# Norm factors of a recurrent attention layer: their rows read ahead of the weight loads, sums of squares taken two pairs at a time, first type's factors applied ahead of the chunk mask

## The chip, the cores and the metric

One NeuronCore of a Trainium2 chip runs the whole program. The time is the device time of one launch in microseconds (us). Before the change three runs took 3392.41, 3395.30 and 3405.55 us, median 3395.3 us.

## The reference, cut to what matters

The layer is x += 0.5 FFN(LN(x)); x += attention(LN(x)); x += 0.5 FFN(LN(x)), for x of 4 sequences x 512 tokens x 256 features. The FFN is a mixture of 64 experts with 8 chosen per token. The change touches only the attention layer, a gated linear recurrence over 64 heads with a state of 128 x 8 per head:

```
Bm = rmsnorm((x @ WB.T)) * Bn_w + B_bias      # 64 heads x 128 entries per token
Cm = rmsnorm((x @ WC.T)) * Cn_w + C_bias      # rmsnorm(v) = v * rsqrt(mean(v*v) + 1e-6), per head
Bm, Cm = rope(Bm, cumsum(theta*dt)), rope(Cm, cumsum(theta*dt))
h_t = alpha_t h_{t-1} + beta_t B_{t-1} x_{t-1} + gamma_t B_t x_t ;   y_t = C_t h_t
y = (y * silu(z)) @ Wout.T
```

B and C are the two "types". Each head of each type needs one norm factor per token, 1/sqrt(mean of squares + eps).

## The kernel before, in words

The program runs the first FFN, then the attention of the four sequences one after the other (scans 0 to 3), and the second FFN. The routing of the second FFN begins between scans. Each scan has a preparation (`prep_*`) and then 32 turns, one for each pair of heads; a turn is one pass of the loop body of `turn_pe`, `turn_act`, `turn_dve`, `turn_pool` and `turn_sp`, written out four times (j = 0 to 3) inside a loop of eight. Each engine runs its own list in a written order, and semaphores tie the lists together: `e_*` are raised by engines and `a_*` by landed DMAs. Work for several pairs is in flight. In turn n, TensorE does in this order: the sums of squares of pair n+2 (`ss_pe`, L1220), the outputs of pair n-2 (`Y_pe`, L1414 and L1416), the chunk products of pair n-1 (`G_pe`, L1350), its transposes (L1359), half of the B/C projection of pair n+3 (`A_pe`, L64), the chunk states of pair n-1 (`K2_pe`, L1390), the other half of the projection, and the angle projection of pair n+2 (`T_pe`, L64). VectorE does: angle scaling (L1171) and scan (L1174) of pair n+1, the decay scan of pair n (L1280), L1285, L1180, then `K_dve1` (the mask on the chunk products, L1374), in odd turns `Y_dve` (L1428, L1432), then `F_dve1` (the norm factors times B, then times C, both L1274), in odd turns `R_dve` (a reciprocal, L1250), the four rope multiplies `F_dve3` (L1298), and the state scan `K_dve2` (L1399). GpSimd follows with L1306 and L1307, which finish the rotated B and C that `G_pe` of the next turn reads.

The norm factors travel once per two pairs. After the second `ss_pe` of a group (odd turn), ScalarE takes the square root (`R_act`, L1238). A DMA turns the 8 rows of 512 into a 128 x 32 tile (`R_rows`, L1245, rc_in), VectorE takes the reciprocal (L1250), a DMA writes it to DRAM (`R_sp2`, L1255, rr_dram), and once that has landed two DMAs read it back, broadcast over the partitions (`R_sp3`, L1264, rr_bc, 2 x 512 KB). The next turn, an even one, begins `F_dve1` with these factors.

All loads of scans 1 to 3 are issued by SP, in one list and on one DMA queue. An odd turn's SP list is: dt rows, end rows (L1149), th load (L1055, 256 KB), wb load (L1047, 1024 KB), `R_rows`, al rows (L1149, 2 x 128 KB), `R_sp2`, `R_sp3`. In scan 0 the weights come from another array, are split into a high and a low part on ScalarE and VectorE, and `R_rows` is issued by ScalarE on its own queue, as in the changed kernel; only L1255 and L1264 are SP's there.

The sums of squares are matmuls of a 128 x 32 one-hot slice with a 128 x 512 tile of squares. Each writes one of two 32-row column groups of one PSUM bank, two matmuls (even and odd entries) for B and two for C per pair. The square root's target, `stdr`, is a slice of the tile `decay_t`.

## Time and profile before

| | |
|---|---|
| median of 3 runs | 3395.3 us (3392.41 to 3405.55) |
| the profiled execution | 3382.4 us, span 3380.6 us |
| granted TensorE clock, mean over the span | 0.909 |
| TensorE busy | 2799.0 us, 83% |
| VectorE busy | 2326.1 us, 69% |
| ScalarE busy | 1816.0 us, 54% |
| GpSimd busy | 1501.2 us, 44% |
| data moved | 609.71 MB, mean 180 GB/s |

The four scans lie from about 590 us to about 2900 us. The mean shares mix them with the two FFNs and with the stretches between scans, so the argument reads the steady part of the scans by itself. Times in timelines are microseconds from the start of the span; DMA rows show when the issuing queue worked, not when the data landed.

### The profile page before, as it was taken

The numbers are of one execution on the slowest core, as the hardware profiler recorded it, in microseconds if no ns is written. First come the engines' busy times: TensorE is split into PE (matmuls) and PEld (weight loads), VectorE is DVE, ScalarE is ACT, GpSimd is POOL, SyncE is SP. The second block draws the span as 40 slices with busy tenths as digits, with TensorE's granted clock in tenths as the row PEclk, the third lists the DMA queues.
The fourth block names the chain that finished last, engine by engine and source line by source line (L and its number), as shares of the span: only waits on it lengthen the run. The fifth ranks groups of instructions, "written<-read, shape, count | busy, mean of one in ns | idle before, by whom it ended". The sixth has DMA issues, their size and how long they took to land.

```text
span 3380.6 us, 83925 instructions
## 1 busy us (share of the span) xinstructions
PE 2799.0 (83%) x28752; PEld 2118.0 (63%) x28752; DVE 2326.1 (69%) x3926; ACT 1816.0 (54%) x3740; POOL 1501.2 (44%) x1354
## 2 busy tenths in 40 slices
PE   4229997789999789999977999998899998549990
PEld 3118885466666557777754677776577776438870
DVE  5205354789999479999855999994799997324364
ACT  1006654577777167666514777763677774126650
POOL 2470155344444344455500666662456665340256
PEclk7559998899999799999978999999999999669995
DMA  9737896556665255566404666652566662548893
GB/s 389 239 131 233 261 296 200 169 181 198 209 192 179 91 158 156 166 172 173 114 1 127 184 175 169 177 152 63 173 179 182 178 174 77 216 138 256 281 288 118
DMA packets 315367, 609.71 MB, mean 180 GB/s; under 512 B 59152, under 2 KB 163728, under 8 KB 314128
## 3 DMA queue, kind: packets, MB, share of 16 engines
q1 hardware_dynamic: 272352, 501.29, 49.3%
q0 software_dynamic: 24576, 67.14, 6.2%
q10 hardware_dynamic: 18224, 38.54, 3.0%
q8 instruction: 120, 1.97, 0.2%
q14 instruction: 95, 0.78, 0.1%
HBM read 446.25 MB, written 159.51 MB: 179 GB/s over the span
## 4 chain that ended last, share of the span: by engine, by line
PE 63%; DVE 8%; ACT 7%; issue 7%; another core or an unknown queue 6%; DMA 5%; POOL 2%; ACTq 1%; SPq 1%; DVEq 0%; POOLq 0%
PE bank L64 23%; PE bank L572 6%; PE bank L1220 6%; PE bank L1350 4%; PE bank L1414 3%; PE bank L1390 3%; PE bank L1416 3%; PE bank L563 2%; PE cs_sn L586 2%; ACT btr L1365 2%; PE bank L1359 2%; PE bank L586 2%; DMA xl<-xd 1%; ACT sq L1231 1%
## 5 line engine op out<-in xcount | busy, mean ns | idle before, releaser
L64 PE MATMUL bank<-xh,wb 128*128 128x512 f32 x2048 | 677.7, 412 | 71.4 <-ACT btr L1365 37.8
L64 PEld LDWEIGHTS bank<-xh,wb 128*128 128x128 f32 x2048 | 367.6, 189 | 188.6 <-ACT btr L1365 58.1
L1229 ACT ACTIVATE xbc<-bank,norm_w 128x512 f32<-128x512 f32 x512 | 350.7, 685 | 234.0 <-PE bank L64 227.5
L1306 POOL TENSOR_TENSOR rot<-rot,tmp 128x512 f32<-128x512 f32 x256 | 330.7, 1292 | 204.0 <-DVE tmp L1298 204.0
L64 PE MATMUL bank<-xl,wb 128*128 128x512 f32 x1024 | 406.6, 397 | 0.0
L572 PE MATMUL bank<-wgu,xgT 128*128 (+1 forms) x1536 | 327.2, 337 | 92.0 <-issue 71.9
L648 DVE TENSOR_TENSOR hh<-sg,bank 128x96 f32<-128x96 f32 x384 | 97.5, 254 | 408.7 <-ACT sg L622 212.8
L1318 POOL TENSOR_TENSOR sq<-cst,rho 128x512 f32<-128x512 f32 x128 | 133.6, 1044 | 494.7 <-DVE xbc L1274 275.1
L1307 POOL TENSOR_TENSOR rot<-rot,tmp 128x512 f32<-128x512 f32 x256 | 331.4, 1295 | 0.0
L1298 DVE SCALAR_TENSOR_TENSOR rot<-xbc,bias,cs_sn 128x1024 f32<-128x1024 f32 x256 | 325.4, 1271 | 8.6 <-DVE xbc L1274 6.8
L1298 DVE SCALAR_TENSOR_TENSOR tmp<-xbc,bias,cs_sn 128x1024 f32<-128x1024 f32 x256 | 326.1, 1274 | 0.0
L1323 POOL TENSOR_TENSOR xc<-xc,sq 128x512 f32<-128x512 f32 x128 | 163.4, 1276 | 358.0 <-DVE xwp L1285 354.6
L1274 DVE TENSOR_TENSOR xbc<-xbc,rr_bc 128x1024 f32<-128x1024 f32 x256 | 308.0, 1244 | 5.7 <-DMA rr_bc<-rr_dram 3.7
L572 PEld LDWEIGHTS bank<-wgu,xgT 128*128 128x128 f32 x1536 | 249.2, 196 | 97.3 <-issue 96.2
L1231 ACT ACTIVATE sq<-bank 128x512 f32<-128x512 f32 x512 | 303.8, 593 | 4.1 <-PE bank L1220 3.1
L1220 PE MATMUL bank<-sq,cst 128*32 128x512 f32 x1024 | 245.3, 600 | 31.8 <-ACT sq L1231 31.0
L1365 ACT ACTIVATE btr<-bank 128x512 f32<-128x512 f32 x256 | 140.3, 595 | 232.5 <-PE bank L1359 230.5
L1416 PE MATMUL bank<-st,rot 128*64 128x16 f32 x3584 | 243.5, 214 | 0.0
L1416 PEld LDWEIGHTS bank<-st,rot 128*64 128x64 f32 x3584 | 230.9, 144 | 0.0
L64 PEld LDWEIGHTS bank<-xl,wb 128*128 128x128 f32 x1024 | 193.7, 189 | 47.9
L1414 PEld LDWEIGHTS bank<-x1p,sq 128*64 128x64 f32 x2048 | 135.5, 143 | 134.8 <-issue 116.7
L616 ACT ACTIVATE xgT<-bank 128x256 f32<-128x256 f32 x384 | 145.8, 380 | 120.2 <-remote 44.2
(293 smaller groups left out, 5840.3 us busy)
## 6 DMA issues: line engine op xcount, KB each, us to landing
wb<-watt_dram SPq DMA_DIRECT2D x96, 1024.0 KB
rr_bc<-rr_dram SPq DMA_DIRECT2D x128, 512.0 KB, 6.5
yd<-ys SPq DMA_DIRECT2D x96, 512.0 KB
wd<-w_down SPq DMA_DIRECT2D x384, 96.0 KB
dt_bc<-row_dram SPq DMA_DIRECT2D x256, 128.0 KB
al_bc<-row_dram SPq DMA_DIRECT2D x256, 128.0 KB
watt_dram<-wb ACTq DMA_DIRECT2D x29, 1024.0 KB, 5.2
xd<-xg SPq DMA_DIRECT2D x12, 2048.0 KB, 23.8
```

Of the source, the lines that this page charges most:

```text
L64: ins = e.matmul(dst, a, m, start=start and c == 0, stop=stop and c == n - 1, skip_group_check=not (start and stop))
L572: ins = e.matmul(gub[n % 2][:, 0:NI2], xgT[n % 3][:, k, :], w, start=k == 0, stop=k == KD - 1)
L1220: ins = e.matmul(SSB[32 * ty:32 * ty + 32, :], one_hot[:, first:first + 32], sq4[:, 2 * ty + eo, :], start=j % 2 == 0 and eo == 0, stop=j ...
L1229: e.activation(xbc[j % 4][:, i, :], of(i)[:, :], ACT.Copy, scale=norm_w[:, i:i + 1])
L1231: e.activation(sq4[:, i, :], of(i)[:, :], ACT.Square).then_inc(e_X.sem, 1)
L1274: e.tensor_tensor(both, both, r.unsqueeze(1).to_broadcast([P, 2, SEQ]), ALU.mult).then_inc(dst.sem, 1)
L1298: ins = e.scalar_tensor_tensor(o[:, 2 * ty:2 * ty + 2, :], X[:, i, :].unsqueeze(1).to_broadcast([P, 2, SEQ]), bias_of(i), cs_sn[:, :, :], ...
L1306: e.tensor_tensor(R[:, 2 * ty, :], R[:, 2 * ty, :], tmp[:, 2 * ty + 1, :], ALU.subtract)
L1307: ins = e.tensor_tensor(R[:, 2 * ty + 1, :], R[:, 2 * ty + 1, :], tmp[:, 2 * ty, :], ALU.add)
L1365: e.activation(btr[:, eo, :], XBANK[x][:, :], ACT.Copy).then_inc(e_bt.sem, 1)
L1414: e.matmul(o, m1[:, (a * TT + t) * CL:(a * TT + t + 1) * CL], c4(x1p[j][:, :])[:, a * TT + t], start=True, stop=True)
L1416: ins = e.matmul(y[CL:P, k, w:w + PW].rearrange("p (a d) -> p a d", a=2), R[:, 2 + eo, CL * k:CL * k + CL], hist[:, eo, :, :, k], start=eo ...
```

## The change

`ss_pe` does nothing for the first pair of a group but wait for the squares, and for the second pair it issues eight matmuls instead of four, for both pairs, into four column groups. The squares get two buffers (`sq4[j % 2]`), and the square root a tile of its own with 128 partitions; its 8 rows now lie in two blocks of 4, so `R_rows` is two DMAs. In scans 1 to 3 `R_rows` stands on SP ahead of the th and wb loads. `F_dve1` is cut in two: B's factors are multiplied ahead of `K_dve1`, C's stay where both were.

```diff
         def ss_pe(e, m, j):
+            e.wait_ge(e_X.sem, e_X.at(4 * (m + 1)))
             if j % 2 == 0:
-                e.wait_ge(e_sr.sem, e_sr.at(m // 2 if isinstance(m, int) else m >> 1))
-            e.wait_ge(e_X.sem, e_X.at(4 * (m + 1)))
+                e.nop(nofuse=True)
+                return
+            e.wait_ge(e_sr.sem, e_sr.at(half(m)))
             for eo in range(2):
-                for ty in range(2):
-                    first = 30 - 28 * (1 - ty) - 2 * (j % 2)
-                    ins = e.matmul(SSB[32 * ty:32 * ty + 32, :], one_hot[:, first:first + 32], sq4[:, 2 * ty + eo, :],
-                                   start=j % 2 == 0 and eo == 0, stop=j % 2 == 1 and eo == 1, skip_group_check=True)
+                for g in range(4):
+                    first = 30 * (g % 2)
+                    ins = e.matmul(SSB[32 * g:32 * g + 32, :], one_hot[:, first:first + 32], sq4[g % 2][:, 2 * (g // 2) + eo, :],
+                                   start=eo == 0, stop=eo == 1, skip_group_check=True)
...
-                e.wait_ge(e_ssm.sem, e_ssm.at(m))
-                e.activation(sq4[:, i, :], of(i)[:, :], ACT.Square).then_inc(e_X.sem, 1)
+                e.wait_ge(e_ssm.sem, e_ssm.at(half(m)))
+                e.activation(sq4[j % 2][:, i, :], of(i)[:, :], ACT.Square).then_inc(e_X.sem, 1)
...
-            e.activation(stdr, SSB[0:36, :], ACT.Sqrt, scale=1.0 / NS, bias=eps_nm[0:36, 0:1]).then_inc(e_sr.sem, 1)
+            e.activation(stdr[:, :], SSB[:, :], ACT.Sqrt, scale=1.0 / NS, bias=eps_nm[:, 0:1]).then_inc(e_sr.sem, 1)
...
-            e.dma_start(rc_in[:, :], stdr[NORM_ROWS, :].rearrange("r (c w) -> r c w", w=32)).then_inc(a_r1.sem, 16)
+            for h in range(2):
+                e.dma_start(rc_in[CL * h:CL * h + CL, :], stdr[CL * h + 30:CL * h + 34, :].rearrange("r (c w) -> r c w", w=32)).then_inc(a_r1.sem, 16)
...
                 if T:
                     T_dve2(e, n + 1, j + 1)
+                F_dve1(e, n, j, b * NB + it + 1, [0])
                 if K:
                     K_dve1(e, p, jp)
                 if j % 2 == 1 and not (first and j == 1):
                     Y_dve(e, n - 2, q - 3, b * (NP // 2) + it * 2 + (j - 3) // 2, n + 1 + T)
-                F_dve1(e, n, j, b * NB + it + 1)
+                F_dve1(e, n, j, b * NB + it + 1, [1])
...
                     end_sp(e, q + 2, j + 2)
+                if RG and not is_first(b):
+                    R_rows(e, gm + 1)
                 if not (last and j >= 1):
                     e.wait_ge(e_th.sem, e_th.at(n + 2))
                     e.nop(nofuse=True)
...
                     if not is_first(b):
                         wb_load_sp(e, b, q + 4, j)
-                if RG and not is_first(b):
-                    R_rows(e, gm + 1)
```

## Rows read from the trace of the kernel before

**Rows 1.** The page's chain of waits, whole span: share by engine.
```profile
PE 63%; DVE 8%; ACT 7%; issue 7%; another core or an unknown queue 6%; DMA 5%; POOL 2%; ACTq 1%; SPq 1%; DVEq 0%; POOLq 0%
```

**Rows 2.** Stretches of scans 3 and 0: length, engines' busy us, clock, DMA share, GB/s.
```profile
2430.00:2810.00 380.00, 372.83 (x4880) 274.80 (x4879) 348.30 (x445) 274.15 (x500) 233.78 (x210) 1.00 0.62 175
760.00:1090.00 330.00, 302.17 (x3936) 220.67 (x3936) 309.84 (x400) 236.48 (x422) 155.57 (x127) 1.00 0.65 198
```

**Rows 3.** VectorE's waits, 2430 to 2810: for whom, us in total, times, longest.
```profile
DVE bank L1171 <- PE bank L64: 10.3, 13, 1.2
DVE sq L1374 <- PE bank L1350: 7.7, 17, 0.5
DVE rc L1250 <- DMA rc_in<-decay_t: 5.8, 9, 1.1
```

**Rows 4.** TensorE's timeline, sums of squares of one turn: start, us.
```profile
2552.08 1.91 PE L1220 MATMUL bank<-sq,cst 128*32 128x512 f32 x8
```

**Rows 5.** VectorE's timeline, an odd turn (2552.32) and an even turn (2567.37).
```profile
2552.32 0.70 DVE L1171 SCALAR_TENSOR_TENSOR bank<-bank,dt_bc 128x512 f32<-128x512 f32 x1 [1.07 <-PE bank L64]
...
2561.41 0.35 DVE L1250 RECIPROCAL rc<-rc_in 128x32 f32<-128x32 f32 x1 [0.19 <-DMA rc_in<-decay_t]
...
2567.37 0.70 DVE L1171 SCALAR_TENSOR_TENSOR bank<-bank,dt_bc 128x512 f32<-128x512 f32 x1
...
2571.43 0.75 DVE L1374 TENSOR_TENSOR sq<-bank,xc 128x256 f32<-128x256 f32 x2
2572.09 2.46 DVE L1274 TENSOR_TENSOR xbc<-xbc,rr_bc 128x1024 f32<-128x1024 f32 x2
...
2579.48 0.84 DVE L1399 TENSOR_TENSOR_SCAN st<-end_bc,bank 64x128 f32<-64x128 f32 x2
2581.27 0.70 DVE L1171 SCALAR_TENSOR_TENSOR bank<-bank,dt_bc 128x512 f32<-128x512 f32 x1 [0.94 <-PE bank L64]
```

**Rows 6.** GpSimd's timeline, end of the odd turn's rope.
```profile
2568.03 1.28 POOL L1307 TENSOR_TENSOR rot<-rot,tmp 128x512 f32<-128x512 f32 x1
```

**Rows 7.** SP's timeline in the odd turn: DMA issues, start and us.
```profile
2552.89 0.58 SPq L1055 DMA_DIRECT2D th<-watt_dram  x1
2553.79 0.57 SPq L1047 DMA_DIRECT2D wb<-watt_dram  x1
2557.13 0.69 SPq L1245 DMA_DIRECT2D rc_in<-decay_t  x1
2558.06 1.21 SPq L1149 DMA_DIRECT2D al_bc<-row_dram  x2
2561.84 0.32 SPq L1255 DMA_DIRECT2D rr_dram<-rc  x1
2563.45 1.29 SPq L1264 DMA_DIRECT2D rr_bc<-rr_dram  x2
```

**Rows 8.** Stretches of the same odd turn; the last two columns are DMA's.
```profile
2554.00:2561.00 7.00, 6.75 (x128) 5.69 (x128) 6.22 (x11) 4.94 (x8) 2.43 (x3) 1.00 0.75 241
2561.00:2565.00 4.00, 4.00 (x45) 3.38 (x45) 3.81 (x5) 3.97 (x8) 1.76 (x2) 1.00 0.08 17
```

**Rows 9.** Tile rr_bc, 2430 to 2810: issue of one DMA to landing.
```profile
DMA to landing us min/median/max: 4.8/5.8/7.2
```

**Rows 10.** SP's waits: two of 2430 to 2810, then one of 820 to 1070.
```profile
SPq L1242 <- ACT decay_t L1238: 29.6, 13, 3.1
...
SPq L1259 <- DMA rr_dram<-rc: 14.2, 13, 1.6
...
SPq L1259 <- DMA rr_dram<-rc: 34.7, 9, 4.0
```

**Rows 11.** Scan 0: VectorE's odd turns and SP's broadcast issue between them.
```profile
899.41 0.70 DVE L1171 SCALAR_TENSOR_TENSOR bank<-bank,dt_bc 128x512 f32<-128x512 f32 x1 [1.10 <-PE bank L64]
...
913.91 1.29 SPq L1264 DMA_DIRECT2D rr_bc<-rr_dram  x2
...
930.48 0.70 DVE L1171 SCALAR_TENSOR_TENSOR bank<-bank,dt_bc 128x512 f32<-128x512 f32 x1 [1.01 <-PE bank L64]
```

More of the change, by code:

```diff
@@ L162, in build @@
         ths, nfr = (sb(n, [P, SEQ]) for n in ("ths", "nfr"))
-        sq4 = sb("sq4", [P, 4, SEQ])
+        sq4 = [sb(f"sq4_{i}", [P, 4, SEQ]) for i in range(2)]
+        stdr = sb("stdr", [P, SEQ])
         btr = sb("btr", [P, 2, SEQ])
@@ L186, in build @@
         norm_w = sb("norm_w", [P, 4])
-        stdr = decay_t[0:36, :, :, :].rearrange("p k q a -> p (k q a)")
-        NORM_ROWS = slice(28, 36)
         rc_in, rc = sb("rc_in", [P, 32]), sb("rc", [P, 32])
@@ L209, in build @@
         coef = tmp[:, 3, TT * NH:].rearrange("p (t n) -> p t n", t=TT)
-        silu_z = [sq4[:, f, :] for f in range(KI)]
+        silu_z = [sq4[0][:, f, :] for f in range(KI)]
         gated = rot[1]
@@ L1211, in A_pe @@
                              True, True).then_inc(e_pj.sem, 1)
+        half = lambda m: m // 2 if isinstance(m, int) else m >> 1
         def ss_pe(e, m, j):
+            e.wait_ge(e_X.sem, e_X.at(4 * (m + 1)))
             if j % 2 == 0:
-                e.wait_ge(e_sr.sem, e_sr.at(m // 2 if isinstance(m, int) else m >> 1))
-            e.wait_ge(e_X.sem, e_X.at(4 * (m + 1)))
+                e.nop(nofuse=True)
+                return
+            e.wait_ge(e_sr.sem, e_sr.at(half(m)))
             for eo in range(2):
-                for ty in range(2):
-                    first = 30 - 28 * (1 - ty) - 2 * (j % 2)
-                    ins = e.matmul(SSB[32 * ty:32 * ty + 32, :], one_hot[:, first:first + 32], sq4[:, 2 * ty + eo, :],
-                                   start=j % 2 == 0 and eo == 0, stop=j % 2 == 1 and eo == 1, skip_group_check=True)
+                for g in range(4):
+                    first = 30 * (g % 2)
+                    ins = e.matmul(SSB[32 * g:32 * g + 32, :], one_hot[:, first:first + 32], sq4[g % 2][:, 2 * (g // 2) + eo, :],
+                                   start=eo == 0, stop=eo == 1, skip_group_check=True)
             ins.then_inc(e_ssm.sem, 1)
@@ L1229, in A_act @@
                 e.activation(xbc[j % 4][:, i, :], of(i)[:, :], ACT.Copy, scale=norm_w[:, i:i + 1])
-                e.wait_ge(e_ssm.sem, e_ssm.at(m))
-                e.activation(sq4[:, i, :], of(i)[:, :], ACT.Square).then_inc(e_X.sem, 1)
+                e.wait_ge(e_ssm.sem, e_ssm.at(half(m)))
+                e.activation(sq4[j % 2][:, i, :], of(i)[:, :], ACT.Square).then_inc(e_X.sem, 1)
         e_rc = ev("e_rc")
         def R_act(e, gm):
-            e.wait_ge(e_ssm.sem, e_ssm.at(2 * (gm + 1)))
-            e.wait_ge(a_r1.sem, a_r1.at(gm))
-            e.activation(stdr, SSB[0:36, :], ACT.Sqrt, scale=1.0 / NS, bias=eps_nm[0:36, 0:1]).then_inc(e_sr.sem, 1)
+            e.wait_ge(e_ssm.sem, e_ssm.at(gm + 1))
+            e.wait_ge(a_r1.sem, a_r1.at(2 * gm))
+            e.activation(stdr[:, :], SSB[:, :], ACT.Sqrt, scale=1.0 / NS, bias=eps_nm[:, 0:1]).then_inc(e_sr.sem, 1)
         def R_rows(e, gm):
@@ L1244, in R_rows @@
             e.nop(nofuse=True)
-            e.dma_start(rc_in[:, :], stdr[NORM_ROWS, :].rearrange("r (c w) -> r c w", w=32)).then_inc(a_r1.sem, 16)
+            for h in range(2):
+                e.dma_start(rc_in[CL * h:CL * h + CL, :], stdr[CL * h + 30:CL * h + 34, :].rearrange("r (c w) -> r c w", w=32)).then_inc(a_r1.sem, 16)
         def R_dve(e, gm):
-            e.wait_ge(a_r1.sem, a_r1.at(gm + 1))
+            e.wait_ge(a_r1.sem, a_r1.at(2 * (gm + 1)))
             e.wait_ge(a_r2.sem, a_r2.at(gm))
@@ L1264, in R_sp3, with F_dve1 @@
                 e.dma_start(rr_bc[par][CL * a:CL * a + CL, :, :], src.to_broadcast([CL, 4, SEQ])).then_inc(a_rr[par].sem, 16)
-        def F_dve1(e, n, j, cnt):
+        def F_dve1(e, n, j, cnt, types):
             e.wait_ge(e_X.sem, e_X.at(4 * (n + 1)))
             par = (j // 2) % 2
-            if j % 2 == 0:
+            if j % 2 == 0 and 0 in types:
                 e.wait_ge(a_rr[par].sem, a_rr[par].at(2 * cnt))
             for ty, dst in ((0, e_xb), (1, e_xcc)):
+                if ty not in types:
+                    continue
                 r = rr_bc[par][:, 2 * ty + j % 2, :]
@@ L1704, in z_act @@
         def z_act(e, b, f):
-            e.wait_ge(e_ssm.sem, e_ssm.at((b + 1) * NP))
+            e.wait_ge(e_ssm.sem, e_ssm.at((b + 1) * (NP // 2)))
             e.wait_ge(e_z.sem, e_z.at(KI * b + f + 1))
```

## The prediction

> **What bounds the kernel now.** I read the chain of waits first: the reader is to see that TensorE holds 63% of it [rows 1]. Then the steady stretches: in scan 3 TensorE is busy 372.83 of 380 us at granted clock 1.00 (2.4 GHz), VectorE 348.30 of 380 [rows 2]. So both are nearly full, and what one gives up the other soon takes back. VectorE's waits say how much room there is: 10.3 + 7.7 + 5.8 = 23.8 us in 380 us [rows 3]. Two turns take 28.95 us (2552.32 to 2581.27 [rows 5]), so 380 us hold 13.1 of them and VectorE waits 1.8 us in each. That is the ceiling of any gain that leaves VectorE's work alone, as this change does. Last I followed the norm factors through VectorE and SP over one odd and one even turn [rows 5 to 8], because the change moves a DMA past two others there.
>
> I count from the start of an odd turn on VectorE, 0 = 2552.32. Its square root is done and `R_rows` issued at 4.8 (2557.13), the reciprocal runs at 9.1 (2561.41), rr_dram is written at 9.5, rr_bc is issued at 11.1. The second of its two issues begins about 0.65 later and lands 4.8 to 7.2 after that [rows 9]: 16.6 to 19.0. The even turn starts at 15.05 (2567.37) and needs rr_bc at 19.8 (2572.09). The margin is 1 to 3 us, and VectorE does not wait.
>
> **Sums of squares.** Before, a turn spends 1.91 us on four matmuls, 3.8 us per two turns [rows 4]. Two column groups run side by side there; if four do, eight matmuls take 1.9 us, and if they don't, 3.8. No row shows four groups at work, so these are the ends: TensorE gives up 1.9 us per two turns or nothing. I take 1.9. The Trainium skill, "TensorEngine Tiling (Array Packing)", section Tiling Modes, lists 128 rows x 32 columns as four tiles that work in parallel; by that the value is 1.9, which no run here shows yet. All of it falls in the even turn. There `G_pe` also needs the rotated pair from GpSimd, ready at 2569.31 (2568.03 + 1.28 [rows 6]), 1.94 after the even turn starts. Before, the mask followed the products at 2571.43 [rows 5], and the products took some 1.2 us, so they started at 2570.2. TensorE can start them at about 2569.4, so 0.8 to 1.0 us is real. That just removes the 0.94 to 1.07 us that VectorE waits at the next turn's start [rows 5].
>
> **B's factors ahead of the mask.** The multiply costs 1.2 us in either place (2.46 for both [rows 5]). It fills the 7.7 us of waits for the products: 0.6 per two turns. The mask comes 1.2 us later, which the state matmuls don't feel, since half a projection (3 us) lies before them. Double-buffered squares and a square root over 128 instead of 36 partitions: nothing, the free size stays 512. The price of the split is that rr_bc is needed earlier: where the mask started, 4.06 after the even turn starts (2571.43 - 2567.37), no longer at 4.72.
>
> If factors were never late, two turns would then take VectorE's work plus remnants: 28.95 - 1.0 - 0.5 = 27.5 us. The even turn would begin at about 14.4 and need rr_bc at 14.4 + 4.06 = 18.5.
>
> **Rows ahead of the loads.** This is where I expect the loss. SP waits for the square root at `R_rows` already now, 29.6 us in 13 times, 2.3 each [rows 10]; th and wb are issued before that wait. After the change they stand behind it. `R_rows` starts at 4.8 as before, since the square root follows VectorE's scan and a table load, not SP. Its two DMAs take 0.5 to 0.7 each (one of twice the size takes 0.69 [rows 7]), so th is issued at about 6.3, wb at 7.2, al at 8.1 to 9.3, against 0.6, 1.5 and 5.7 now. What is queued behind: `R_sp2` at 9.5, which is when it was issued before (SP frees at 9.3; the reciprocal is done at about 8.8, its old wait of 5.8 us in 380 gone, which gives nothing since SP isn't free). But rr_dram's 16 KB now sit on the queue behind th, wb and al, 1.57 MB by their shapes, where before these had drained: DMA moved 241 GB/s until 2561.0 and 17 GB/s after [rows 8], and rr_dram landed in time for `R_sp3` to issue 1.6 us later.
>
> That a small DMA waits for the big ones ahead is in the rows: rc_in, 16 KB, was issued at 2557.13 behind wb and VectorE waited for it until 2561.41, 4.2 us; rr_dram, the same size, with a drained queue, cost a wait of 1.1 us (14.2/13). In scan 0, where stores and loads are in flight at that time, the same wait is 3.9 us (34.7/9) [rows 7, 10].
>
> When does it land? From th's issue at 2552.89 to the end of the traffic at 2561.0 are 8.1 us; so 6.3 + 8.1 = 14.4, and 0.6 for the write itself: 15.0. Lower end: 1.3 us until data flows (2552.89 to about 2554.2) and 1.57 MB at 270 GB/s (somewhat above the 241 of [rows 8]): 6.3 + 1.3 + 5.8 = 13.4. Upper end: 16.2, if the even turn's stream is already as slow as scan 0's. Then 0.2 to issue, 0.65 to the second rr_bc, 5.8 to 7.2 to land (I take 6.5): 15.0 + 7.35 = 22.4, ends 20.1 and 24.2. VectorE wants it at 18.5: a stall of 3.9 us in each even turn that starts a group.
>
> From there VectorE has B's factors 1.2, mask 0.75, then C's factors to the state scan's end (2572.09 to 2580.32 less one multiply, 7.0): 8.9 us. TensorE isn't later: its state matmuls start after the mask, and 5.5 us on it has ended the angle projection, at 22.4 + 7.6. Two turns take 22.4 + 8.9 = 31.3 us instead of 28.95: +2.35 us. There are 16 groups in a scan, one of them formed in the preparation (its list is not reordered), so 45 in scans 1 to 3: 45 x 2.35 = +106 us. With the ends 20.1 and 24.2 it is 0 and +187 us. The delayed wb load itself is not felt: issued at 7.2, landed by 15, needed by the even turn's projection after 18.
>
> **Scan 0.** `R_rows` stays on ScalarE's queue. Two turns take 31.07 us (899.41 to 930.48 [rows 11]). rr_bc, issued at 913.91, lands about 920.4 to 921.7, and after the change is wanted at about 920.6 where it was wanted at 921.4. So the time of a group is tied to the landing: 21.5 + 8.9 = 30.4 at best. The gain is 0 to 0.7 us in 15 groups; I take 5 us in all. The preparations gain about 1 us together.
>
> **Sum.** +106 - 5 - 1 = +100 us on the profiled execution of 3382.4 us, thus 3482 us. The median of the runs shown is 12.9 us above that execution, so I forecast 3395.3 + 100 = 3495 us.
>
> **Rivals.** *The queue doesn't hold rr_dram back* (the engines take it beside wb). For it: in the even turn the DMA share is full and all still lands. Against: rc_in's 4.2 us. Then rr_bc is there by 18.5 or shortly after, two turns take 27.5 to 27.9 us, and 45 x 1.25 + 10 = 65 us are gained: 3330 us. This is the other side; it decides where rr_dram lands before about 11 (20.1 - 7.35 = 12.8 is the point of no change). Chance 0.09.
>
> *The loads drain much faster than in the odd turn shown*, so that rr_dram lands near 12.8 and stall and saving cancel: 3395 us, within 0.5%; a little faster, 3365, if it lands at 12. For it: short slices move more than 241 GB/s. Against: the seven-microsecond mean of the very same transfers. Chance 0.11, of which 0.08 is no change. "DMA: Bandwidth & Descriptors" of the Trainium skill, section Specifications, gives a fabric ceiling of 435 GB/s; by that the 1.57 MB would take 3.6 us (an estimate from the page), and the time would be some 3360 us. The trace has 241 GB/s for these transfers and disagrees.
>
> *Column groups don't run four abreast*: TensorE keeps its 3.8 us. In the forecast this costs nothing, as TensorE ends the even turn 1.3 us before VectorE and has 5.3 us of VectorE's work before the mask to cover 3.7 + 1.4 + 1.2; it would only turn the first rival into no change. It is not a case of its own.
>
> *TensorE falls to its lower level in the new gaps* of some 3 us per two turns, or later loads are late as well: 3580 us and more, 0.03.
>
> **How the numbers follow.** The forecast holds 0.77 with its own range 3430 to 3565; with the last rival, slower has 0.80. The measurement tells about 0.5% (17 us) from no change. Faster has 0.09 + 0.03 = 0.12, the same 0.08. The range that holds 8 in 10 reaches down to the case of no change: 3400 to 3565.
>
> **What would show it.** VectorE waiting 3 to 5 us for rr_bc at its first multiply of even turns in scans 1 to 3, SP waiting 5 us and more for rr_dram instead of 1.1, th and wb issued 5.7 us later in odd turns, no wait for rc_in, two turns of some 31 us; in scan 0 31 us or slightly less; the squares' matmuls of 1.9 us once per two turns. Wrong if SP's wait for rr_dram stays at 1 to 2 us: then two turns of 27.5 to 28 us, and the kernel is faster.

## The result: 5.6% slower, 3395.3 to 3586.9 us

The changed kernel takes 3586.93 us (median of 3 runs, 3581.56 to 3592.52) against 3395.3 us; the ratio is 1.0557, with a 95% interval of 1.0514 to 1.06. The profiled execution is the one of 3586.93 us, with a span of 3585.1 us; before it was 3382.4 us with a span of 3380.6. The forecast of 3495 us (3400 to 3565) had the direction and about half of the size: 191.6 us came where 100 were forecast, and the time lies outside the range.

**Where the time lies.** From the first to the last prefix-scan input on VectorE, the four scans take 493.2, 499.5, 504.7 and 505.7 us, against 482.2, 443.6, 440.6 and 439.9. That is +11.0 in scan 0 and +185.8 in scans 1 to 3, together 196.8 of the 204.5 us by which the span grew. The length of two turns below is a mean over 12 pairs of turns in one scan, or over all 36 in scans 1 to 3 (from the starts of the line that opens VectorE's turn). It went from 29.0 to 33.6 us in scans 1 to 3.

The profile after. The page's chain of waits first, by engine and then by line:

```profile
PE 33%; DMA 20%; DVE 14%; issue 11%; ACT 8%; another core or an unknown queue 6%; SPq 6%; ACTq 1%; DVEq 0%; POOL 0%; POOLq 0%
PE bank L64 9%; DMA rr_bc<-rr_dram 9%; DMA rr_dram<-rc 7%; PE bank L571 5%; PE bank L1396 2%; PE bank L562 2%; PE cs_sn L585 2%; ACT L1241 2%; PE bank L585 2%; DMA xh<-xd 2%; DVE cum L1173 1%; DVE xbc L1280 1%; DVE tmp L1304 1%; SPq L1148 1%
```

In [rows 1] TensorE held 63% and DMA 5%. Now 16% of the span is two small transfers: rr_dram, and rr_bc that reads it. The chain follows the norm factors from VectorE's scan through ScalarE's square root, SP's issues and two DMAs back to VectorE.

Twelve pairs of turns in scan 3 as one stretch (length, busy us of TensorE, its weight loads, VectorE, ScalarE and GpSimd, granted clock, DMA share, GB/s):

```profile
2569.00:2973.00 404.00, 354.53 (x4456) 275.69 (x4456) 325.33 (x409) 249.13 (x455) 216.72 (x194) 0.90 0.53 153
```

Against [rows 2] VectorE is busy 81% instead of 92%, and the clock is 0.90 where it was 1.00. TensorE's 88% is flattering: it includes instructions made longer by the lower clock. The waits in the same stretch (us in total, times, longest), of VectorE, TensorE and SP in turn:

```profile
DVE xbc L1280 <- DMA rr_bc<-rr_dram: 53.1, 12, 5.9
DVE bank L1170 <- PE bank L64: 18.1, 11, 2.0
...
PE bank L1396 <- DVE sq L1380: 32.0, 11, 3.8
...
SPq L1263 <- DMA rr_dram<-rc: 58.1, 12, 5.5
```

VectorE waits for rr_bc in every pair, 4.4 us each. Its waits for the products and for rc_in [rows 3] are gone, but the one for TensorE's projection at the start of a turn is larger than before (18.1 us in 12 pairs; it was 10.3 in 13), though TensorE was given less to do. TensorE itself now waits for the mask before the state matmuls, 11 times 2.9 us; between 2430 and 2810 the kernel before has no such wait. SP waits 4.8 us for rr_dram where it waited 1.1 [rows 10].

One pair on VectorE, an even turn (2683.13), an odd one (2702.56) and the start of the next (2717.43); start, us, and in brackets the idle time ahead:

```profile
2683.13 0.70 DVE L1170 SCALAR_TENSOR_TENSOR bank<-bank,dt_bc 128x512 f32<-128x512 f32 x1
...
2691.80 1.23 DVE L1280 TENSOR_TENSOR xbc<-xbc,rr_bc 128x1024 f32<-128x1024 f32 x1 [4.61 <-DMA rr_bc<-rr_dram]
...
2702.56 0.70 DVE L1170 SCALAR_TENSOR_TENSOR bank<-bank,dt_bc 128x512 f32<-128x512 f32 x1 [1.96 <-PE bank L64]
...
2706.53 1.98 DVE L1280 TENSOR_TENSOR xbc<-xbc,rr_bc 128x1024 f32<-128x1024 f32 x1
...
2717.43 0.70 DVE L1170 SCALAR_TENSOR_TENSOR bank<-bank,dt_bc 128x512 f32<-128x512 f32 x1
```

Three things differ from [rows 5]: 4.61 us of idle for rr_bc, 1.96 us at the end of the even turn for TensorE, and the odd turn's multiply of B, 1.98 us instead of 1.23. That last one runs beside this GpSimd instruction:

```profile
2706.16 1.27 POOL L1329 TENSOR_TENSOR xc<-xc,sq 128x512 f32<-128x512 f32 x1 [3.59 <-DVE xwp L1291]
```

The chain of waits through that pair and the odd turn ahead of it, which starts at 2668.26 (start, us, what):

```profile
2668.26 0.71 DVE bank L1170
...
2673.14 0.64 SPq L1249
...
2674.75 0.62 SPq L1054
...
2675.71 0.59 SPq L1046
...
2677.84 6.30 DMA rr_dram<-rc
...
2685.01 6.70 DMA rr_bc<-rr_dram
...
2693.84 1.70 PE bank L1396 x32
2695.54 6.87 PE bank L64 x18
```

In the kernel before the same chain has these lengths for the same two groups of matmuls:

```profile
2546.72 1.03 PE bank L1390 x32
2547.76 4.40 PE bank L64 x18
```

The stretches of 1 us around the gap (columns as above) say why they are longer:

```profile
2691.00:2692.00 1.00, 0.00 (x0) 0.00 (x0) 0.20 (x1) 1.00 (x2) 0.00 (x0) 1.00 1.09 232
...
2695.00:2696.00 1.00, 1.00 (x12) 0.94 (x11) 1.00 (x1) 0.00 (x0) 0.85 (x1) 0.50 1.00 391
...
2700.00:2701.00 1.00, 1.00 (x4) 0.81 (x3) 0.59 (x2) 0.00 (x1) 1.00 (x2) 0.54 0.00 0
```

TensorE idles for 3.2 us until the mask is there (its timeline: 3.17), and when it starts again the granted clock falls to 0.50 (1.2 GHz) and stays there for some 7 us (0.54 is the stretch in which it rises again); the state matmuls and the projection behind them take 8.6 us instead of 5.4.

### The profile page after: what moved, and what is told of

Read it like the earlier page. It is cut to its first block, busy times and chain, and to the rows that moved or that the text cites. A ratio compares the mean times of both kernels' runs of the same rounds, so it can differ in the third digit from the quotient of the medians.

```text
span 3585.1 us, 84063 instructions
## 1 busy us (share of the span) xinstructions
PE 2826.0 (79%) x28752; PEld 2214.9 (62%) x28752; DVE 2367.9 (66%) x3926; ACT 1814.7 (51%) x3740; POOL 1505.8 (42%) x1354
## 4 chain that ended last, share of the span: by engine, by line
PE 33%; DMA 20%; DVE 14%; issue 11%; ACT 8%; another core or an unknown queue 6%; SPq 6%; ACTq 1%; DVEq 0%; POOL 0%; POOLq 0%
PE bank L64 9%; DMA rr_bc<-rr_dram 9%; DMA rr_dram<-rc 7%; PE bank L571 5%; PE bank L1396 2%; PE bank L562 2%; PE cs_sn L585 2%; ACT L1241 2%; PE bank L585 2%; DMA xh<-xd 2%; DVE cum L1173 1%; DVE xbc L1280 1%; DVE tmp L1304 1%; SPq L1148 1%
## 5 line engine op out<-in xcount | busy, mean ns | idle before, releaser
L64 PE MATMUL bank<-xh,wb 128*128 128x512 f32 x2048 | 737.9, 444 | 84.1 <-ACT btr L1371 42.8
L64 PEld LDWEIGHTS bank<-xh,wb 128*128 128x128 f32 x2048 | 406.3, 209 | 208.3 <-ACT btr L1371 62.1
L1280 DVE TENSOR_TENSOR xbc<-xbc,rr_bc 128x1024 f32<-128x1024 f32 x256 | 368.9, 1442 | 190.1 <-DMA rr_bc<-rr_dram 187.9
L64 PE MATMUL bank<-xl,wb 128*128 128x512 f32 x1024 | 434.1, 424 | 0.0
L1313 POOL TENSOR_TENSOR rot<-rot,tmp 128x512 f32<-128x512 f32 x256 | 330.7, 1292 | 0.0
L1304 DVE SCALAR_TENSOR_TENSOR rot<-xbc,bias,cs_sn 128x1024 f32<-128x1024 f32 x256 | 324.9, 1269 | 8.3 <-DVE xbc L1280 6.5
L1304 DVE SCALAR_TENSOR_TENSOR tmp<-xbc,bias,cs_sn 128x1024 f32<-128x1024 f32 x256 | 326.3, 1275 | 0.0
L1396 PE MATMUL bank<-xwp,btr 128*64 128x16 f32 (+1 forms) x4096 | 163.6, 221 | 117.2 <-DVE sq L1380 111.0
L1396 PEld LDWEIGHTS bank<-xwp,btr 128*64 128x64 f32 x4096 | 153.2, 157 | 166.4 <-issue 155.0
L1422 PE MATMUL bank<-st,rot 128*64 128x16 f32 x3584 | 251.2, 217 | 0.0
L64 PEld LDWEIGHTS bank<-xl,wb 128*128 128x128 f32 x1024 | 212.5, 208 | 54.5
L1422 PEld LDWEIGHTS bank<-st,rot 128*64 128x64 f32 x3584 | 238.5, 148 | 0.0
```

The source lines that it names most:

```text
L64: ins = e.matmul(dst, a, m, start=start and c == 0, stop=stop and c == n - 1, skip_group_check=not (start and stop))
L1280: e.tensor_tensor(both, both, r.unsqueeze(1).to_broadcast([P, 2, SEQ]), ALU.mult).then_inc(dst.sem, 1)
L1304: ins = e.scalar_tensor_tensor(o[:, 2 * ty:2 * ty + 2, :], X[:, i, :].unsqueeze(1).to_broadcast([P, 2, SEQ]), bias_of(i), cs_sn[:, :, :], ...
L1313: ins = e.tensor_tensor(R[:, 2 * ty + 1, :], R[:, 2 * ty + 1, :], tmp[:, 2 * ty, :], ALU.add)
L1396: ins = e.matmul(S[h, eo, 2 * t + 1:2 * t + 1 + nk, :], btr[:, eo, t * P + CL * a:t * P + CL * a + CL], i, start=True, stop=True)
L1422: ins = e.matmul(y[CL:P, k, w:w + PW].rearrange("p (a d) -> p a d", a=2), R[:, 2 + eo, CL * k:CL * k + CL], hist[:, eo, :, :, k], start=eo ...
```

## The experiments

The absolute times differ between chips (the kernel before takes 3266 to 3400 us; the difference lies outside the scans, as in h3 and k1, whose spans are 126 us apart and their scans 1 to 3, where they are the same program, 2 us in all), so each row is compared with runs of the kernel before on its own chip. "Low clock" is the time in a pair at which the granted clock was below 1, a mean over the same 36 pairs. "0" and "1 to 3" are scans. All lengths are worked out from starts in each run's one trace.

| Run | What it has | Ratio, 95% interval | Two turns, 1 to 3 | Low clock | Two turns, 0 |
|---|---|---|---|---|---|
| r2_before | kernel before, again | 0.9997 (0.9977 to 1.0017) | 29.00 | 0 | 31.2 |
| r2_after | changed kernel, again | 1.0554 (1.0521 to 1.0588) | 33.25 | 6.0 | 32.2 |
| e4_sums_alone | sums | 1.0048 (1.0031 to 1.0066) | 29.51 | 2.2 | 32.6 |
| e6_split_alone | split | 1.0064 (1.0039 to 1.0089) | 29.56 | 0.2 | 31.5 |
| e2_rows_alone | rows | 1.0205 (1.0182 to 1.0227) | 30.63 | 1.1 | 31.2 |
| e1_rows_back | sums, split | 1.0146 (1.0117 to 1.0174) | 30.10 | 2.8 | 32.2 |
| f1_rows_sums | rows, sums | 1.0301 (1.0265 to 1.0338) | 31.36 | 3.5 | 32.3 |
| f2_rows_split | rows, split | 1.0379 (1.0345 to 1.0413) | 32.07 | 2.1 | 31.4 |
| e5_write_on_act | all, rr_dram on ScalarE's queue | 1.0536 (1.0507 to 1.0564) | 33.20 | 6.0 | 32.2 |
| h4_half_wb | all, half of wb's bytes | 1.0151 (1.0106 to 1.0196) | 30.20 | 2.4 | 32.1 |
| e3_fill | all, 14 fill matmuls | 1.0662 (1.0634 to 1.0691) | 33.33 | 2.7 | 35.6 |
| h1_fill8 | all, 8 fill matmuls, scans 1 to 3 | 1.0441 (1.0399 to 1.0483) | 32.22 | 2.1 | 32.2 |
| e7_sums_rows_act | sums, rows on ScalarE | 1.0159 (1.0127 to 1.0191) | 30.16 | 2.1 | 32.2 |
| e8_sums_fill4 | sums, 4 fill matmuls | 1.0135 (1.011 to 1.016) | 29.34 | 0.8 | 34.1 |
| h2_before_late_recip | before, reciprocal later | 1.0016 (0.9995 to 1.0037) | 28.98 | 0 | 31.3 |
| h3_sums_late_recip | sums, reciprocal later | 1.0025 (1.0 to 1.0049) | 28.72 | 0.7 | 32.8 |
| k1_sums_split_in_scan0 | the same, scan 0's sums per turn | 1.0026 (1.001 to 1.0042) | 28.91 | 1.1 | 32.5 |

### The parts, alone and in pairs

e1_rows_back, the changed kernel with `R_rows` behind wb's load again:
```
-                if RG and not is_first(b):
-                    R_rows(e, gm + 1)
                 if not (last and j >= 1):
...
                     if not is_first(b):
                         wb_load_sp(e, b, q + 4, j)
+                if RG and not is_first(b):
+                    R_rows(e, gm + 1)
```


> The changed kernel with the norms' rows issued on SP behind the wb load again, as before; sums taken two pairs at a time and B's factors ahead of the mask stay. Theory (the small write of the reciprocals waits in SP's ring behind 1.57 MB of loads): the write lands within 1.5 to 2 us, rr_bc lands about 18.6 us after the odd turn's start, wanted at 18.9, so hardly a stall; two turns take 28.0 to 28.8 us instead of 34.2, and the time is 3350 to 3390 us. Rival (it is not the place of the rows but the earlier need of B's factors that makes VectorE wait): VectorE still waits 3 us and more for rr_bc, two turns stay above 31 us, time above 3480 us.

e2_rows_alone is the kernel before with the reverse of this edit and nothing else:

> The kernel before with only the norms' rows moved ahead of the th and wb loads. Theory: rr_bc lands about 23.5 us after the odd turn's start, as in the changed kernel, but the mask is done before VectorE waits, so TensorE has its work and keeps its clock; two turns take 23.5 + 8.1 = 31.6 us, 45 x 2.65 = +119 us, time about 3515 us (3490 to 3540), granted clock near 0.91. Rival (the move is the whole cost): 3570 us and more, clock near 0.87. Second rival (the ring does not matter): 3395 us, SP's wait for rr_dram 1.1 us each.

e4_sums_alone is e1 with B's multiply behind the mask again:
```
-                F_dve1(e, n, j, b * NB + it + 1, [0])
...
-                F_dve1(e, n, j, b * NB + it + 1, [1])
+                F_dve1(e, n, j, b * NB + it + 1, [0, 1])
```


> The changed kernel with the rows behind the wb load again and B's factors again beside C's: what is left of the change is the sums taken two pairs at a time. Theory: TensorE gives up 1.9 us per two turns, VectorE gains back about 1.0 us of its waits; two turns 28.95 -> about 28.0 us, in all four scans, 60 x 0.9 = -54 us, time about 3340 us (3325 to 3360). Rival (what TensorE gives up is hidden, because the next products wait for GpSimd and VectorE anyway): 3395 us within 10.

e6_split_alone is the kernel before with only this edit reversed:

> The kernel before with only the split of the factors' multiply: B's ahead of the mask. Theory (the B multiply now runs beside GpSimd's own two-operand work of L1323 and takes 1.98 instead of 1.22 us, and rr_bc is wanted 0.7 us earlier): VectorE's work grows by 0.75 us a turn, less the 0.25 us a turn that it waited for the products; all four scans longer by 0.4 to 0.8 us a turn, 128 turns, +50 to +100 us, ratio 1.015 to 1.03. Rival (it fills the wait for the products and costs nothing): ratio 0.995 to 1.00.

No part alone makes the kernel faster. Of the six expectations on parts and pairs only that of f1 held, and just: e1, e4 and e6 came between their two theories or beside both, e2 cost less than said (30.6 us for 31.6), and so did f2 (32.1 for 33). The move of the rows costs most: 2.05%. VectorE's waits for rr_bc in 12 pairs of e2's scan 3:

```profile
DVE xbc L1274 <- DMA rr_bc<-rr_dram: 29.6, 12, 4.8
```

The split costs 0.64% though it does what it was for: the wait for the products is not among e6's waits. What it costs is in the multiply itself, 12 pairs of e6 (count | busy, mean ns), then 13 pairs of the kernel before:

```profile
L1276 DVE TENSOR_TENSOR xbc<-xbc,rr_bc 128x1024 f32<-128x1024 f32 x48 | 76.8, 1600 | 0.4
```
```profile
L1274 DVE TENSOR_TENSOR xbc<-xbc,rr_bc 128x1024 f32<-128x1024 f32 x52 | 62.2, 1236 | 0.4
```

Four multiplies per pair: 4 x 0.364 = 1.46 us more, against 1.2 us of waits for products and projection that went, and 0.3 us more wait for rc_in (9.4 us in 12 pairs, against 5.8 in 13).

The sums of squares are grouped as intended: the kernel's eight matmuls, which the trace counts as 16 (and the four of before as eight), take 1.93 us, as long as four took [rows 4]. So four column groups do run at once.

```profile
2702.33 1.93 PE L1223 MATMUL bank<-sq,cst 128*32 128x512 f32 x16
```

The gain of that does not arrive. In 12 pairs of e4's scan 3 the clock is 0.97, and VectorE waits for TensorE, for rc_in and for the products about as long as before:

```profile
2373.00:2725.00 352.00, 330.70 (x4468) 257.05 (x4464) 318.56 (x408) 251.35 (x457) 218.02 (x194) 0.97 0.62 176
```
```profile
DVE bank L1170 <- PE bank L64: 10.2, 12, 2.4
DVE rc L1254 <- DMA rc_in<-stdr: 7.2, 5, 1.9
DVE sq L1380 <- PE bank L1356: 7.2, 13, 0.6
```

Much of what TensorE gave up comes back as a wait of its own. In the same 12 pairs it waits 1.2 us per pair for VectorE's state scan before the outputs of the even turn, where the kernel before has no such wait between 2430 and 2810:

```profile
PE bank L1420 <- DVE st L1405: 14.2, 12, 2.7
```

The long ones (2.0 to 2.7 us) are the four pairs in which VectorE's reciprocal had waited 1.3 us and more for rc_in in the turn ahead. Behind each of them the granted clock falls to 0.50, and in the next pair VectorE waits 1.4 to 2.4 us for TensorE's projection (seen in three; the fourth ends the stretch).

f1_rows_sums is the changed kernel without the split, f2_rows_split the changed kernel with the sums and the single sq4 of before.

> Rows ahead of the loads and sums two pairs at a time, but the factors' multiply in one place behind the mask: the changed kernel without the split. Theory (the late factors cost VectorE 3 to 4 us in either case, but only with B's factors ahead of the mask do they keep TensorE from its state matmuls, so that it idles and its clock falls): TensorE has no gap of 3 us and more, two turns take 30.6 us as with the rows alone plus about 0.5 for falls of the clock that the sums bring, ratio to the kernel before 1.02 to 1.03. Rival (the three parts' costs simply add): two turns about 31.2 us and the ratio near 1.025 too, but then the rows with the split would be 1.027 and the changed kernel 1.032, not 1.056.

> Rows ahead of the loads and B's factors ahead of the mask, but sums for each pair as before: the changed kernel without the grouped sums. Theory: TensorE waits for the mask 2 to 3 us in even turns and its clock falls behind that; two turns 33 us or slightly more, ratio 1.045 to 1.055, half-speed stretches in every pair of turns. Rival (costs add): ratio 1.02 + 0.006 = about 1.027, two turns 31.3 us, no half-speed stretches.

The parts do not add up. Alone they cost 2.05, 0.48 and 0.64%, 3.2% together, and the whole costs 5.5%. The largest excess is in the pair of rows and split: 3.8% where 2.7% is the sum. With the split, the mask stands behind the late multiply, so the wait for rr_bc passes on to TensorE. f2, 12 pairs of scan 3, TensorE's wait before the state matmuls:

```profile
PE bank L1392 <- DVE sq L1376: 25.1, 12, 3.8
```

e2 has no such line: there VectorE's mask comes first, and the state matmuls start on time. r2_before and r2_after repeat both kernels on the chip of f1 and f2:

> The kernel before, unchanged, for a profile on the chip of the experiments. Both theories: ratio 1.00, two turns of scans 1 to 3 take 28.9 to 29.1 us as in the trace before; the feed-forward stretches are shorter than in that trace by what the totals differ, about 115 us.

> The changed kernel, unchanged, on the chip of the experiments. If the scans behave as in its first trace: two turns 33.7 us, ratio 1.05 to 1.06.

### What holds rr_dram: order on a queue, or bytes in flight

e5_write_on_act, the changed kernel with the 16 KB write issued by ScalarE in scans 1 to 3:
```
 # SP
-                    R_sp2(e, gm + 1, (j // 2 + 1) % 2)
+                    if is_first(b):
+                        R_sp2(e, gm + 1, (j // 2 + 1) % 2)
 # ScalarE
+                if RG and not is_first(b):
+                    R_sp2(e, gm + 1, (j // 2 + 1) % 2)
```


> The changed kernel, but in scans 1 to 3 the 16 KB write of the reciprocals (rr_dram) is issued by ScalarE on its own queue, so that it no longer stands behind th, wb and al in SP's ring. Theory (ring order holds it back): it lands about 1.5 us after its issue, some 13 us after the odd turn's start instead of 16; rr_bc's own data still queue behind the loads, so rr_bc lands at about 21 instead of 23.5; two turns lose about 2.5 us, ratio to the kernel before about 1.02 to 1.03 instead of 1.056. Rival (the 16 DMA engines are simply busy, whichever queue the write is on): SP still waits about 5 us for the write, ratio 1.05 to 1.06.

The prediction's picture, rr_dram standing in line behind th, wb and al on SP's queue, says that another queue frees it. It does not: the ratio is 1.0536, and SP's wait before rr_bc in 12 pairs of scan 3 is even longer, 5.9 us (it begins earlier, since SP no longer spends 1.2 us on the issue):

```profile
SPq L1263 <- DMA rr_dram<-rc: 70.7, 12, 6.3
```

One such write in e5's timeline:

```profile
2573.04 0.59 SPq L1046 DMA_DIRECT2D wb<-watt_dram  x1
...
2575.05 0.33 ACTq L1259 DMA_DIRECT2D rr_dram<-rc  x1
...
2581.69 1.28 SPq L1268 DMA_DIRECT2D rr_bc<-rr_dram  x2
```

The write was issued by ScalarE 2.0 us after wb, and rr_bc could be issued only 6.6 us later. From issue to landing rr_dram takes 1.4 us in h2 (below), where nothing is in flight, and 6.1 (median) in the changed kernel, by the view of its tile over 12 pairs each:

```profile
DMA to landing us min/median/max: 1.4/1.4/1.4
```
```profile
L1259 SPq DMA_DIRECT2D rr_dram<-rc x12: 513/1237/1732, 2577.8 to 2947.8; - x12
...
DMA to landing us min/median/max: 4.7/6.1/6.9
```

The Trainium skill, "DMA: Bandwidth & Descriptors", section Queues, rings and completion order, says that the semaphore write of a DMA lands only after every earlier write of that DMA engine, across its queues. That would hold back the notice of a write that is done. Here the write itself is late, so this run does not test the rule. The same pair's DMA packets (queue, packets, MB, share of 16 engines), from the issue to 2578.00 and from there to 2581.00; q1 is SP's queue and q10 ScalarE's:

```profile
q1 hardware_dynamic: 313, 1.08, 95.2%
```
```profile
q1 hardware_dynamic: 110, 0.20, 21.3%
q10 hardware_dynamic: 144, 0.02, 4.8%
```

For 3 us after the issue not one packet of the write moves, while SP's loads fill the engines. Over the 12 pairs its first packet starts 3.0 to 3.4 us after the issue, as it does on SP's queue in the changed kernel (3.0 to 3.4), and 0.8 us after it in h2. What inside the DMA engines sets this order stays open.

h4_half_wb takes half of wb's bytes away (the loads of the turns in scans 1 to 3; the other columns keep older values):
```
-                        wb_load_sp(e, b, q + 4, j)
+                        e.dma_start(wb[j % 2][:, :, 0:BCW // 2].bitcast(F32),
+                                    pair_of(watt_dram, q + 4)[:, :, 0:BCW // 2]).then_inc(a_wb[j % 2].sem, 16)
```


> The changed kernel, but in scans 1 to 3 each turn's load of wb carries half of its columns (the other half keeps older values; the output is not the reference's). Theory (rr_dram's small write waits until the bytes that were issued before it are over, and the gap before the state matmuls then lowers TensorE's clock): a third or more of the bytes in flight goes, about 2 us of the 6; rr_bc lands 2 us earlier, VectorE's wait falls from 4.4 us per two turns to 2.5 or less, the gap before the state matmuls falls from 3 to 4 us to 1 to 2, the clock falls seldom or not at all, the projection behind it is back from 6.9 to 4.4 us, two turns take 29.5 to 31 us instead of 33.4, ratio 1.01 to 1.03. Rival (the wait is a fixed delay of small transfers, whatever the bytes): wait and ratio stay, 1.05 to 1.06. Second rival (bytes matter, the clock doesn't): two turns fall by the 2 us of the wait alone, to 31.4, with the projection unchanged at 6.9 us.

Two turns fall from 33.4 to 30.2 us. Waits of VectorE, TensorE and SP in 12 pairs of scan 3:

```profile
DVE xbc L1280 <- DMA rr_bc<-rr_dram: 29.3, 12, 3.1
...
DVE bank L1170 <- PE bank L64: 0.4, 1, 0.4
...
PE bank L1396 <- DVE sq L1380: 4.5, 6, 1.2
...
SPq L1263 <- DMA rr_dram<-rc: 43.2, 12, 4.1
```

A third of the bytes of th, wb and al is gone; the wait for rr_bc falls by 2.0 us per pair. Of that, 1.2 us is SP's wait for rr_dram (4.8 to 3.6), and 0.7 the issue of the write on SP, whose median is 0.54 us here and 1.24 in the changed kernel (the line of L1259 above; 0.32 before [rows 7]):

```profile
L1259 SPq DMA_DIRECT2D rr_dram<-rc x12: 329/536/543, 2478.4 to 2812.1; - x12
```

TensorE's wait for the mask falls from 2.7 to 0.4 us per pair, and VectorE's wait for TensorE from 1.5 to nothing. So the bytes set the wait, and with a third of them gone two turns are 3.2 us shorter, more than the 2.0 of the wait alone. The fixed delay falls as a theory, and so does the one in which the clock plays no part. But the expectation that the clock seldom falls was wrong: it is low for 2.4 us in a pair still, without making anybody late.

### What the low clock costs

The fill matmuls are the kernel's own `unread` (whole 512-column matmuls whose result nothing reads, 0.25 us each at full clock, not column groups as the second expectation has it), put before the state matmuls of even turns; e3_fill has 14 in all four scans, h1_fill8 has 8 in scans 1 to 3:
```
+                if j % 2 == 0 and not first and not last and not is_first(b):
+                    e.wait_ge(e_sr.sem, e_sr.at(half(n + 2)))
+                    e.nop(nofuse=True)
+                    unread(e, SSB[:, :], 8)
                 if K:
                     K2_pe(e, p, jp)
```


> The changed kernel with 14 unused matmuls (0.21 us each at full clock, about 3 us) on TensorE ahead of the state matmuls of even turns, into the bank of the sums, which is free then; they lie in the gap of 3 to 4 us in which TensorE waits for the mask. Theory (the clock falls to half after that gap and the 18 projection matmuls take 6.9 instead of 4.4 us): clock 1.00 in the steady part, VectorE's wait of 2.0 us for TensorE at odd turns goes, two turns 34.2 -> about 32.4 us, 45 x 1.8 = -80 us, time about 3505 us (3490 to 3530). Rival (TensorE is late for another reason, or the clock does not answer to such filling): 3580 us or more.

> The changed kernel with 8 unused 32-column-group matmuls set before the state matmuls of even turns, in scans 1 to 3 alone, behind a wait for the square root so that they fall into the gap. Theory (the idle before the state matmuls lowers the clock, and the lower clock costs): 1.7 us of the 3 to 4 us gap are filled; half-clock time falls from 65 to 75 us per scan to 20 to 40, two turns from 33.4 to about 32.3, ratio 1.03 to 1.045. Rival (the low clock is a mere companion; VectorE waits for rr_bc either way): no change, 1.05 to 1.06. If the fill itself delays the state matmuls: over 1.06, and the clock stays up nevertheless.

e3 was a miss: 1.0662. In scans 2 and 3 it gained (33.7 to 32.4 us), in scan 1 it lost (33.3 to 35.2; why stays open) and in scan 0, where there is no gap to fill, it cost 3.4 us per pair. h1 is the clean version: 1.0441, whose interval lies below the changed kernel's. One of its gaps, on TensorE's timeline, and then its waits in 12 pairs of scan 3:

```profile
2620.23 2.00 PE L235 MATMUL bank<-every,before 128*128 128x512 f32 x8
2622.16 1.10 PE L1396 MATMUL bank<-xwp,btr 128*64 128x16 f32 x32
```
```profile
DVE xbc L1280 <- DMA rr_bc<-rr_dram: 50.4, 11, 5.5
...
DVE bank L1170 <- PE bank L64: 0.3, 1, 0.3
...
PE bank L1396 <- DVE sq L1380: 10.8, 8, 2.2
```

VectorE waits for rr_bc as long as without the fill (4.6 us each time, against 4.4), so the stall is untouched; the state matmuls are back at 1.1 us, the low clock goes from 6.0 to 2.1 us per pair, and VectorE's wait for TensorE is gone. The lower clock in itself is therefore worth at least 1.0 to 1.35 us per pair (33.25 and 33.57 in the two traces of the changed kernel against 32.22), 1.1% of the time. That useless work makes the kernel faster here is the plainest sign of it.

### Where the sums' gain goes

e7_sums_rows_act is e4 with `R_rows` issued by ScalarE, right behind its square root, in every scan, e8_sums_fill4 is e4 with `unread(e, SSB[:, :], 4)` in the place that the even turn's sums left.

> Sums two pairs at a time, factors' multiply in one place, and the norms' rows issued by ScalarE on its own queue in all scans, which is neither behind nor ahead of the loads on SP. Theory: VectorE's waits for rc_in (up to 1.9 us in an odd turn) go, the clock's falls stay; ratio to the kernel before 0.995 to 1.003 against 1.0048 with the rows on SP. Rival (rc_in's data wait for busy engines on any queue): unchanged, 1.004 to 1.006.

> Sums two pairs at a time alone (rows behind the wb load, multiply in one place) with 4 unused matmuls of 0.21 us in the place from which the even turn's sums were taken. Theory (sums alone gained nothing because TensorE's clock fell to half for 3 to 7 us in every second or fourth turn once the dense 1.9 us of the even turn were gone): the clock stays at 1.00 in the steady scans or nearly, two turns come to about 28.3 us, ratio 0.98 to 0.99. Rival (the clock does not answer to so small a filling): two turns 29.5 us as with sums alone, ratio 1.004 or more.

e7 loses 1.1% to e4, where it was to gain: in 270 us of its scan 3 VectorE waits 11.4 us for rc_in, up to 2.7 at a time, against 7.2 in 352 us of e4. e8 brings the low clock from 2.2 to 0.8 us per pair and gains 0.2 us per pair with it in scans 1 to 3, but loses 1.6 in scan 0. Of the sums' 0.5 us per pair 0.3 are left with the low clock nearly gone, so their loss is not the clock alone, and the expectation of 0.98 to 0.99 was a miss.

h2_before_late_recip and h3_sums_late_recip move VectorE's reciprocal behind the first type of `F_dve3`, in the kernel before and in e4:
```
-                if RG:
-                    R_dve(e, gm + 1)
                 F_dve3(e, n, j, q, [0])
+                if RG:
+                    R_dve(e, gm + 1)
```


> The kernel before with the reciprocal one VectorE operation later, behind the first type of the last multiply. Theory (the wait for rc_in costs 0.5 us per two turns and rr_bc has a margin of 1 to 3 us): the wait goes, rr_bc comes about 0.7 us later and is still in time; two turns 28.5 to 28.95, ratio 0.985 to 1.000. Rival (the margin is gone in part of the pairs): waits for rr_bc appear, ratio 1.000 to 1.010.

> The grouped sums of squares alone (no moved rows, no split), with the reciprocal one VectorE operation later as well. Theory: as beside, the rc_in wait of 0.6 us per two turns goes: 1.005 becomes 0.99 to 1.00. Rival (TensorE's clock, low after every second even turn, sets the pace there): no change, 1.00 to 1.01.

h2 is no different from before (1.0016), as its rival had it: the wait for rc_in is gone, but in 12 pairs of scan 3 there stands

```profile
DVE xbc L1274 <- DMA rr_bc<-rr_dram: 13.3, 12, 1.6
```

1.1 us per pair in its place. The prediction's margin of 1 to 3 us for rr_bc is at its low end: in the trace before, rr_bc lands 1.2 us ahead of the multiply (median of 12 groups, 0.5 to 1.5). In h2 two operations of 1.3 us stand ahead of the reciprocal, not one as the expectation says; it starts 11.3 us after the odd turn's start instead of 9.4, and that uses the margin up. h3 brings scans 1 to 3 to 28.7 us, the best of all kernels, and scan 0 to 32.8. Against e4 that is 0.8 us per pair: with the waits for rc_in TensorE's long waits before its outputs are gone (none over 0.8 us in 12 pairs of scan 3), and the low clock falls from 2.2 to 0.7 us. So in scans 1 to 3 the sums lose by the late rc_in and what follows from it, and without it they gain 0.3 us per pair; the rest of the 1.9 us stays hidden. k1_sums_split_in_scan0 gives scan 0 its matmuls back in each turn:
```
+            if j % 2 == 0 or not each_turn:
+                e.wait_ge(e_sr.sem, e_sr.at(half(m)))
             for eo in range(2):
-                for g in range(4):
+                for g in ((0, 1, 2, 3) if not each_turn else (j % 2, 2 + j % 2)):
```


> The grouped sums with the later reciprocal, but in scan 0 four of the eight matmuls of the sums stand in each turn, as in the kernel before. Theory (in scan 0 the loss comes from the even turn's missing matmuls, after which TensorE's clock falls): scan 0's two turns go back from 32.35 to about 31.15, its length from 499.6 to about 479 us, scans 1 to 3 stay at 28.5 to 28.9; ratio 1.0025 becomes about 0.996 to 0.998, perhaps the first version ahead of the kernel before, though hardly beyond what the measurement can tell. Rival (the loss in scan 0 comes from the double-buffered squares or from the order of the square root's inputs, not from the clock): scan 0 stays at 32.3, ratio 1.002.

That theory fell. Scan 0's low clock goes from 6.0 to 0.9 us per pair, but its two turns stay at 32.5. VectorE's and TensorE's waits in its 12 pairs:

```profile
DVE sq L1383 <- PE bank L1359: 12.7, 10, 2.5
...
PE bank L1224 <- ACT sq L1237: 24.3, 20, 1.9
```

TensorE waits for ScalarE's squares 20 times where it did 15 times before, and the products are late for the mask. Every kernel with the two-buffer sums has this slower scan 0 (32.1 to 32.8 without fill matmuls, against 31.2 to 31.5), whatever its clock. Which of their edits does it (the second buffer of squares, the square root over 128 partitions, the two DMAs for rc_in) stays open. No version that was run beats the kernel before.

## Why the prediction was half right

**The stall was right, in place and nearly in size.** From the start of an odd turn on VectorE (2668.26 in the trace after), as forecast and measured: rc_in issued at 4.8, 4.9; rr_dram landed at 15.0 (13.4 to 16.2), 15.9; rr_bc landed at 22.4 (20.1 to 24.2), 23.5; wanted at 18.5, 18.9; wait 3.9, 4.4 over 12 pairs. VectorE's work from there to the state scan's end: 8.9, 8.8. The attributed cause was not right in one respect: it is not SP's queue that holds the write, for it is held on another queue too (e5); it is the bytes in flight (h4). The sum did not suffer, because it only asked when the loads are through. One reading was loose: rc_in was used 4.3 us after its issue, but VectorE waited for it for only 0.19 us of that [rows 5].

**"TensorE isn't later: its state matmuls start after the mask, and 5.5 us on it has ended the angle projection" failed.** This is the main error. The working took 5.5 us from before; after a gap of some 3 us the clock is at 1.2 GHz, and state matmuls and projection take 8.6 us. TensorE, said to end 1.3 us before VectorE, ends 1.96 after it. The rival that named the clock got a chance of 0.03, with "3580 us and more".

**"The multiply costs 1.2 in either place" failed.** At its new place in the odd turn it takes 1.98 us beside GpSimd's two-operand instruction, in e6 in both turns. That is 0.7 us per pair of the changed kernel and 1.46 of e6. The Trainium skill, "SBUF — State Buffer", section Who interferes with whom, has the rule: a VectorE instruction with two SBUF inputs reads the second through an interface that it shares with GpSimd, and whoever comes later is blocked. The trace fits it, roughly: GpSimd's instruction ends at 2707.43, 0.90 us after VectorE's record began, and 1.08 us on the multiply ends, where a whole one takes 1.23. The rope multiplies (L1304), whose second tensor lies in PSUM, keep their 1.27 us beside GpSimd's two-operand L1313 (2698.57 and 2698.78 in the same trace). No run moved GpSimd's instruction away, so this cause rests on the overlap. The row of GpSimd's instruction should have been laid beside the new place.

**The sums' gain of 0.8 to 1.0 us failed**, while the 1.93 us for 16 matmuls held. Alone, the sums make two turns 0.5 us longer. The working let TensorE go on to the products at once; the outputs ahead of them need VectorE's state scan, and TensorE waits there for 1.2 us per pair (e4).

Per pair of scan 3, against the forecast's +2.35 us (31.3 - 28.95), the growth is 33.67 - 28.95 = +4.7. In terms, from [rows 2, 3] with 13.1 pairs and the waits after with 12:

| Term, us per pair | forecast | measured |
|---|---|---|
| wait for rr_bc | +3.9 | 53.1/12 = +4.4 |
| VectorE's wait for TensorE | -1.0 | 18.1/12 - 10.3/13.1 = +0.7 |
| wait for the products | -0.5 | -0.6 |
| wait for rc_in | 0 | -0.4 |
| the multiplies, 4 x (1.412 - 1.236) | 0 | +0.7 |
| sum | +2.4 | +4.8 |

The mean after of 1.412 us is from the same 12 pairs:

```profile
L1280 DVE TENSOR_TENSOR xbc<-xbc,rr_bc 128x1024 f32<-128x1024 f32 x48 | 67.8, 1412 | 53.5 <-DMA rr_bc<-rr_dram 53.1
```

Scans 1 to 3 grew by 185.8 us, that is 41 pairs of 4.56 us (the mean of the 36, 33.57 - 29.01), where the forecast took 45: the pairs at a scan's ends aren't like the others. Against the forecast scans 1 to 3 are 80 us longer (185.8 for 106) and scan 0 is 16.

**Scan 0: -5 forecast, +11 measured.** The gain had to come from the sums, and all kernels with them lose there.

**What would show it.** The signs named came true: th and wb 6 us later in odd turns (2674.75 and 2675.71, 6.5 and 7.5 after the start, against 0.6 and 1.5 [rows 5, 7]), SP's wait of 5 us for rr_dram, VectorE's of 3 to 5 for rr_bc, none for rc_in. The two turns of some 31 us did not come (33.6), and the missing sign was one about TensorE's clock.
